# The last norm's statistics on ScalarE with running sums, and x added on TensorE by a product with the identity

## The reference

```
delta  = max(softplus(x @ W_delta.T), 1e-4);  decay = exp(-delta * sigmoid(log_a))
update = sigmoid(x @ W_select.T) * tanh(x @ W_in.T);  gate = sigmoid(x @ W_gate.T)
state_t = decay_t * state_{t-1} + update_t
x1 = layernorm(x + (gate * state) @ W_out.T)          # over the 128 channels

xn = batchnorm(x1) * gamma + beta                     # over all tokens
q  = xn @ w_q.T ;  sim = q against keys: 2 x 8 heads x 32 keys
top 8 of 32 for each half, top 8 of the 8 x 8 sums -> 8 of 1024 experts per head
o  = gelu(x1 . key_in[expert]) * softmax(scores)
y  = sum over heads and experts of o * key_out[expert]
out = layernorm(x1 + y)                               # over the 128 channels
```

## Time and profile before

| what | value |
|---|---|
| median of 3 runs | 532.36 us (530.75 to 534.48) |
| profiled execution | 531.46 us, span 529.7 us |
| busy in the span | PE 369.5, PEld 270.4, DVE 444.1, ACT 236.2, POOL 220.0 us |
| mean granted clock of TensorE | 0.768 of full |
| chain that ended last | PE 52%, DVE 20%, issue 17%, ACT 8% |
| DVE waits for `listsT` | 26.6 us in 9 waits |
| idle before scatter's matmuls, no releaser | 70.0 us in 38 pauses |

### The profile page before, as it was taken

The page is one execution under the profiler, slowest core; times in us unless marked ns, Lnnn a source line. Parts: engine busy times, 40 slices in busy tenths (PEclk is TensorE's granted clock), DMA queues, the critical chain, the costliest instruction groups (busy, mean ns, idle before and its releaser), DMA issues.

```text
span 529.7 us, 24223 instructions
## 1 busy us (share of the span) xinstructions
PE 369.5 (70%) x10097; PEld 270.4 (51%) x10097; DVE 444.1 (84%) x2770; ACT 236.2 (45%) x371; POOL 220.0 (42%) x311
## 2 busy tenths in 40 slices
PE   5686786418537775786777787847976876778856
PEld 2233474114434555464736484726464656556855
DVE  1537899699999969898999699989998997998643
ACT  3967804426514532463346235632644372345212
POOL 1042420144348751616283428435252747082630
PEclk9989965759655876898778668876886796588878
DMA  8700000000000000000000000000000000000001
GB/s 236 165 0 2 1 1 0 1 1 2 4 2 5 3 2 4 3 4 4 24 2 4 4 24 3 4 22 5 2 5 24 5 3 4 22 4 2 24 6 41
DMA packets 7661, 8.95 MB, mean 17 GB/s; under 512 B 896, under 2 KB 6912, under 8 KB 7424
## 3 DMA queue, kind: packets, MB, share of 16 engines
q1 hardware_dynamic: 6976, 7.34, 5.1%
q10 hardware_dynamic: 576, 0.07, 0.1%
HBM read 5.31 MB, written 2.10 MB: 14 GB/s over the span
## 4 chain that ended last, share of the span: by engine, by line
PE 52%; DVE 20%; issue 17%; ACT 8%; DMA 1%; SPq 0%; ACTq 0%; DVEq 0%
PE psum L880 17%; PE psum L857 16%; PE psum L867 9%; PE psum L837 5%; PE psum L776 4%; DVE arena L669 3%; DVE idx L614 3%; DVE arena L525 2%; DVE x L575 2%; ACT L423 1%; DVE vals L606 1%; DVE arena L673 1%; DVE arena L666 1%; DVE arena L672 1%; DVE picked L638 1%
## 5 line engine op out<-in xcount | busy, mean ns | idle before, releaser
L857 PE MATMUL psum<-arena 64*64 64x16 f16 x8192 | 93.8, 182 | 91.5 <-issue 70.0
L857 PEld LDWEIGHTS psum<-arena 64*64 64x64 f16 x8192 | 87.7, 120 | 110.0 <-issue 104.8
L880 PE MATMUL psum<-ko,arena 64*128 64x128 f32 x1024 | 91.2, 355 | 3.6 <-issue 3.6
L417 ACT ACTIVATE arena<-psum 128x1024 f32<-128x1024 f32 x32 | 32.8, 1024 | 134.0 <-PE psum L857 134.0
L880 PEld LDWEIGHTS psum<-ko,arena 64*128 64x128 f32 x1024 | 88.0, 267 | 4.2 <-issue 3.9
L239 POOL TENSOR_TENSOR cand<-vals 128x128 f32<-128x128 f32 x16 | 13.2, 824 | 169.1 <-DVE vals L606 169.1
L614 DVE FIND_INDEX8 idx<-vals,sims 128x8 uint32<-128x32 f32 x512 | 82.7, 185 | 0.0
L286 POOL TENSOR_TENSOR arena<-arena 128x512 f32<-128x512 f32 x60 | 77.8, 1331 | 4.2 <-ACT arena L417 4.2
L669 DVE TENSOR_TENSOR arena<-iota,listsT 128x4096 f16<-128x4096 f16 x32 | 74.9, 2341 | 0.0
L867 PE MATMUL psum<-x1T,trn 128*64 128x256 f32 x512 | 62.8, 400 | 8.7 <-ACT arena L423 8.7
L837 PE MATMUL psum<-msim,xn 128*128 128x512 f32 x64 | 54.9, 1008 | 4.9 <-ACT xn L375 4.9
(11 more groups left out here) (113 smaller groups left out, 529.5 us busy)
## 6 DMA issues: line engine op xcount, KB each, us to landing
x<-in_L_attn_x_dram SPq DMA_DIRECT2D x8, 256.0 KB, 4.7
out_dram<-nat SPq DMA_DIRECT2D x7, 256.0 KB, 2.3
ko<-in_L_ffn_key_out_dram SPq DMA_DIRECT2D x2, 512.0 KB, 9.5
nat<-in_L_ffn_key_in_dram SPq DMA_DIRECT2D x2, 256.0 KB, 8.0
nat<-in_L_ffn_keys_dram SPq DMA_DIRECT2D x2, 128.0 KB, 5.4
out_dram<-nat SPq DMA_DIRECT2D x2, 128.0 KB, 1.7
nat<-in_L_attn_W_delta_dram SPq DMA_DIRECT2D x1, 64.0 KB, 2.8
nat<-in_L_attn_W_in_dram SPq DMA_DIRECT2D x1, 64.0 KB, 2.7
```

The lines of the kernel that those rows point to most:

```text
L417: act.activation(dst, src, ACT.Copy, scale=1.0 / W_SCALE).then_inc(s["p_evac"], 1)
L857: end = pe.matmul(psum[64 * e:64 * e + 64, at:at + NJ], hotx[rows, g, :, e], hotw[rows, part, g, :, e], start=(part == 0), stop=(part == 1))
L880: end = pe.matmul(y2[:, e, m % 2] if m < NS - 1 else y_last[:, e], gl[rows, m % 4, j, :], ko[rows, j, :], start=(j == 0), stop=(j == NJ - 1))
```

## The change

DVE loses `residual` and `last_residual`. x1 enters on PE: `experts_out` begins with two f32 products of x1T (128 rows) with the identity, which open the accumulation; the 32 products with key_out then add to it. ACT gets three things. `z_out(q)`, behind `lists_out` in odd steps from m = 5, copies four tiles of `y2` to `zf` with Identity and sums each row on the way. `centred`, called by `spread2`, behind `gelus`, multiplies the sums by -1/D, takes Square of `zf` with that as bias and sums again, and takes the root of the sum of squares over D. For the last chunk both are called in halves. DVE's `scales` uses `nm2` for the mean.

```diff
+            def summed(tiles, src):
+                for t in tiles:
+                    end = act.activation(zf[:, t, :], src(t), ACT.Identity, accum_out=sum2[:, t:t + 1])
+                end.then_inc(s["zf_done"], 1)
+            def z_out(q):
+                wait(act, "y2_mm", q * 2 + 2)
+                wait(act, "out_done", q)
+                summed(range(CH), lambda t: y2[:, t % 2, t // 2])
+            def centred(tiles, n):
+                lo, hi = tiles[0], tiles[-1] + 1
+                wait(act, "zf_done", n)
+                wait(act, "nmr2_done", n - 1)
+                act.mul(nm2[:, lo:hi], sum2[:, lo:hi], -1.0 / D).then_inc(s["nm2_done"], 1)
+                wait(act, "nm2_done", n)
+                for t in tiles:
+                    end = act.activation(dev2[:, t, :], zf[:, t, :], ACT.Square, bias=nm2[:, t:t + 1],
+                                         accum_out=ssq2[:, t:t + 1])
+                end.then_inc(s["ssq2_done"], 1)
+                wait(act, "ssq2_done", n)
+                wait(act, "out_done", min(n, NCH) - 1)
+                act.activation(rstd2[:, lo:hi], ssq2[:, lo:hi], ACT.Sqrt, bias=eps[:, 0:1],
+                               scale=1.0 / D).then_inc(s["sd2"], 1)
             def spread2(q):
-                wait(act, "mv2_done", q + 1)
-                wait(act, "nmr2_done", q)
-                wait(act, "out_done", q)
-                act.activation(rstd2[:, :], mv2[:, :, 1], ACT.Sqrt, bias=eps[:, 0:1]).then_inc(s["sd2"], 1)
+                centred(range(CH), q + 1)
...
             def spread2_half(u):
-                act.wait_ge(s["mv2_done"], NCH + u)
+                act.wait_ge(s["y2_mm"], NS - 1 + u)
                 act.wait_ge(s["out_done"], NCH - 1)
+                tiles = range(2 * u, 2 * u + 2)
+                summed(tiles, lambda t: y2[:, t % 2, 0] if u == 0 else y_last[:, t % 2])
+                centred(tiles, NCH + u)
...
                 if 1 <= m < NS:
                     lists_out(m - 1)
+                if m >= 5 and m % 2:
+                    z_out(m // 2 - 2)
                 if m + 1 < NS:
                     sims_out(m + 1)
...
+            z_out(NCH - 2)
             spread2(NCH - 2)
...
             def scales(q):
-                dve.scalar_tensor_tensor(out=nmr2[:, :], in0=mv2[:, :, 0], scalar=-1.0, in1=rstd2[:, :],
-                                         op0=ALU.mult, op1=ALU.mult).then_inc(s["nmr2_done"], 1)
+                dve.tensor_tensor(nmr2[:, :], nm2[:, :], rstd2[:, :], ALU.mult).then_inc(s["nmr2_done"], 1)
...
-                    if m >= 5 and m % 2:
-                        residual(m // 2 - 2)
...
             def experts_out(m):
                 wait(pe, "zf_done", m // 2)
+                to = y2[:, :, m % 2] if m < NS - 1 else y_last
+                for e in range(2):
+                    pe.matmul(to[:, e], x1T[:, m * SW + e * P:m * SW + (e + 1) * P], ident[:, :], start=True, stop=False)
                 for j in range(NJ):
...
-                        end = pe.matmul(y2[:, e, m % 2] if m < NS - 1 else y_last[:, e], gl[rows, m % 4, j, :], ko[rows, j, :], start=(j == 0),
-                                        stop=(j == NJ - 1))
+                        end = pe.matmul(to[:, e], gl[rows, m % 4, j, :], ko[rows, j, :], start=False, stop=(j == NJ - 1))
```

More of the change, by code:

```diff
@@ L124, in seqffn_kernel @@
         zf = nat[:, 0:CH, :]
-        st2 = sb("st2", [P, CH, 6])
-        mv2 = sb("mv2", [P, CH, 2])
+        sum2 = sb("sum2", [P, CH])
+        nm2 = sb("nm2", [P, CH])
+        ssq2 = sb("ssq2", [P, CH])
+        dev2 = sb("dev2", [P, CH, P])
         rstd2 = sb("rstd2", [P, CH])
@@ L156, in seqffn_kernel @@
             wk_done whi_done wlo_done conv_done lists_mm lists_evac hoty_done hot_done
-            p_mm p_evac g_mm gelu_done a_done a_tail y2_mm zf_done st2_done mv2_done sd2 rstd2_done nmr2_done
+            p_mm p_evac g_mm gelu_done a_done a_tail y2_mm zf_done nm2_done ssq2_done sd2 rstd2_done nmr2_done
             out_done stored""".split()
@@ L441, in spread2_half @@
             def spread2_half(u):
-                n = slice(2 * u, 2 * u + 2)
-                act.wait_ge(s["mv2_done"], NCH + u)
+                act.wait_ge(s["y2_mm"], NS - 1 + u)
                 act.wait_ge(s["out_done"], NCH - 1)
-                act.activation(rstd2[:, n], mv2[:, n, 1], ACT.Sqrt, bias=eps[:, 0:1]).then_inc(s["sd2"], 1)
+                tiles = range(2 * u, 2 * u + 2)
+                summed(tiles, lambda t: y2[:, t % 2, 0] if u == 0 else y_last[:, t % 2])
+                centred(tiles, NCH + u)
             def norm_out_half(u):
@@ L673, in hots_of @@
                 dve.tensor_tensor(hotw[:, 1, at], hoty[:, at], spread(3, NJ), ALU.mult).then_inc(s["hot_done"], 1)
[L675 to L688, removed]
             def scales(q):
@@ L713, in _ @@
                     hots_of(m - 1, 1)
[L715 to L728, removed]
             def last_scales(u):
@@ L734, in last_scales @@
                 dve.wait_ge(s["rstd2_done"], NCH + u)
-                dve.scalar_tensor_tensor(out=nmr2[:, n], in0=mv2[:, n, 0], scalar=-1.0, in1=rstd2[:, n],
-                                         op0=ALU.mult, op1=ALU.mult).then_inc(s["nmr2_done"], 1)
-            residual(NCH - 2)
+                dve.tensor_tensor(nmr2[:, n], nm2[:, n], rstd2[:, n], ALU.mult).then_inc(s["nmr2_done"], 1)
             dve.wait_ge(s["gelu_done"], NCH * JR)
@@ L748, in _ @@
             for u in range(2):
-                last_residual(u)
                 last_scales(u)
```

## The result

The changed kernel took 545.35 us (median of 4, 541.1 to 546.19) against 533.36 for the kernel before in the same comparison: ratio 1.0248, 95% interval 1.0189 to 1.0306, some 13 us. 547.5 was forecast, 540 to 557. The ratios leave out runs more than 1.5% above the fastest of their kernel, while the medians are of all runs, and the two can differ by about 0.5%.

A forecast was written before the change was run, and what follows sets the result against it. The prediction took PE's chain of work, not DVE, to bound the kernel. PE 11.2, `z_out` 2, late `pack` 0.7 and tail 1.3 summed to 15.2 us over the median 532.36, giving 547.5 us, range 540 to 557.

The forecast's parts named there:

- What bounds the kernel: In the loop PE's order of work sets the pace; work taken off DVE lies ahead of its `listsT` wait, gaining nothing.
- Onto PE: At the head of `experts_out`, 16 uncovered pairs of identity products at 0.70 us add 11.2 us (9.1 to 13.3).
- The bound of 0.83: Price of two identity products in `experts_out`, from five `project_out` products at a low clock taking 2.07 us.
- wrong if the clock rose and gave the 11 us back: Sign of error: PE's granted clock, 0.77 on the mean, rises with the added work and returns the 11 us.
- The pauses: PE's idle without releaser before scatter matmuls, 70.0 us in 38 pauses: change 0, with 3 us either way.
- rival 2: PE's pauses take in the new products; only ACT's share and the tail remain, 4 us: 536.5 us, chance 0.10.
- `z_out`: On ACT before the gelu table load in odd steps: 2.0 us a call, mostly hidden, 2 us in all (0 to 6).
- The late `pack`: ACT's work behind `gelus` delays `signs`, so DVE's `pack` comes 2.9 us later; cost 0.7 us in all (0 to 3.7).
- DVE's busy time: Profile sign: DVE's busy time falls by about 15 us, while its wait for `listsT` or `signs` grows by more.
- The tail: After PE's last product, ACT's 2.5 us replaces 1.25 us: +1.3 us (0.5 to 2.5).
- Table loads for Square: On ACT, Square might want a table of its own, a load of 1.28 us, seven times.
- rival 3: ACT becomes the bound in odd steps, first gelu 1.5 us late a pair, `pack` 5: 556 us, chance 0.18.

The follow-up runs named there:

- PE's part alone: Kernel before plus the two identity products at the head of each `experts_out`, DVE copying y2 to `zf` instead of adding: 541.05 us, ratio 1.0169.
- the kernel with turns: Changed kernel with x1T transposed in TensorE's transpose mode instead of by f32 products with the identity: 534.72 us, ratio 1.0084 to the kernel before.
- the other kernel: Changed kernel with `signs` put ahead of `spread2` on ACT in odd steps: 541.84 us, ratio 1.0166; repeated 542.57 us, ratio 1.0217.

## Why the prediction was right, and where it was off

- **What bounds the kernel: right.** PE's order of work sets the pace in the loop and DVE's 84% do not. Taking 1.1 us a pair from DVE with nothing added changed nothing (0.9995), and the whole move without the products, late `pack` included, gained nothing either (1.0006 and 1.0069). The Trainium skill ("Perfetto Trace Analysis", Identifying the Most-Contended Engine), which by occupancy would name DVE, did not hold here; the waits did.
- **Onto PE: the sum right, its two halves wrong.** 11.2 us was forecast, 9 to 10 measured alone and 11.4 read in the trace. But 0.70 a pair was taken near rows of mean clock; most pairs stand where the clock is low and take 1.22, 17.3 us in all, and 5.9 us come back in the products behind them. The bound of 0.83 from the earlier trace rows was too low for the place: in that stretch the mean granted clock was 0.61, not 0.50. The forecast said it would be wrong if the clock rose and gave the 11 us back: it gave back 5.9 us, nearly all of the 6.1 by which the head went over the forecast, and the mean clock stayed at 0.767. The sum was right by two misses that cancel, and that was luck: the forecast had no reason for either. Afterwards a reason can be given, that added work is in effect paid at the higher clock (16 times 0.71 us), but it is a reading of the traces.
- **The pauses: right.** 38 pauses of 71.8 us in all after, 38 of 70.0 before; rival 2 is excluded by PE's part alone.
- **`z_out`: mis-sized.** The term said 2.0 us a call and 2 us in all; it took 1.0 us a call, and PE's wait for the gelus went from 8.7 to 9.2. Idle before the gelu table load hid it, as the prediction's lower end had it. The copy itself is 0.290 us. The figures of the Trainium skill ("ScalarE: Activation LUTs", What ACT_TABLE_LOAD costs), 186 ns and 0.833 ns a column, give an estimate of 0.293; the trace agrees. The read of a sum starts before the copy's record has ended, so the two cost 0.25 back to back.
- **The late `pack`: the mechanism right, the price not settled.** `pack` waits for `signs` by 2.9 to 5.5 us, where 2 to 3 was forecast, and PE's later waits for the one-hots grow. The term was 0.7 us (0 to 3.7). Exchanging the two calls gives 2.6 and 4.4 us, and 1 us in the kernel with turns; the traces show 1.0 to 1.8 of it. So 0.7 was probably too little, but no comparison excludes it.
- **DVE's busy time: mis-sized.** About 15 us less was forecast, and it was 8.1. The term left out that DVE's own products take longer beside GpSimd's. It cost nothing here, as DVE is not the bound.
- **The tail: half.** From PE's last product to the last scaled tile it was 2.98 us before and is 3.45 now, +0.5 for +1.3.
- Table loads for Square, and ACT as the bound (rival 3): not seen; PE's wait for gelus grew by 0.5 us in all.

With the measured terms, 10 for the products, 0.5 for `z_out`, 1 to 4 for `pack` and 0.5 for the tail, the sum is 12 to 15 us, where 15.2 was forecast and 13 measured.

## What to carry to other kernels

Work that is taken from the busiest engine is worth nothing if that engine then waits for another one; look at what ends its next wait, and put nothing on that engine. When work is added where TensorE's clock is low, look at the records behind it too: here the added products looked dear (1.22 us a pair), and those behind them became cheaper. A wait that a trace names is worth its length only if nothing else would have held the engine: in the last step the wait for the one-hots stands where the other kernel has a pause of the same length. To tell the two apart, compare when the awaited work ended with when the engine went on.

## What the runs showed of the hardware

- A pair of f32 products of 128 by 128 by 128 takes 1.22 us at a granted clock of 0.50 (1.01 after a pause) and 0.71 at 1.00; a pair of turns in transpose mode 0.69 at 0.50 and 0.44 at 1.00 (10 and 5 of 16 places), and products may add onto a turned tile in the same accumulation.
- Over the 16 calls of `experts_out` TensorE stood at 1.2 GHz for 64.5 us before, 63.7 with the new products and 63.2 with twice the products, though the calls took 95.0, 101.4 and 109.7 us.
- A running sum on ScalarE is a second record of 0.19 to 0.22 us that mostly overlaps the ACTIVATE: 0.25 us from start to start for a 128-column copy without pointers, 0.39 for a Square with a pointer bias.
- GpSimd's f32 and VectorE's f16 products slow each other when they run together: from 1.24 to 1.98 us on the mean for one 128 by 512 product on GpSimd, from 0.68 to 1.76 for one of 128 by 1024 on VectorE and from 2.28 to 3.35 for one of 128 by 4096.
